# Round one of a two-branch attention kernel: the second tile's queries and chosen columns formed before the transposed queries, and three weight splits placed behind evacuations

## The reference

```python
xn = layernorm(x)
# branch 1: local attention, 16 query heads, 4 key heads, 32 wide
q, k, v = xn @ Wq.T + bq, xn @ Wk.T + bk, xn @ Wv.T + bv
q, k = rope(rmsnorm(q) * qn_w), rope(rmsnorm(k) * kn_w)
a = softmax(where(key > query or query - key > 64, -10000, q @ k.T * scale)) @ v
out1 = a @ Wo.T + bo
# branch 2: one shared key and value per token, chosen by a gate among 16 heads
gate = softmax(xn @ W_gate.T); idx = argmax(gate)
fq, fk, fv = split(xn @ W_qkv.T)
K, V = fk[head idx], fv[head idx] * max(gate)
out2 = softmax(causal(fq @ K.T / sqrt(32))) @ V      # 16 query heads
return x + out1 + out2
```

## Time and profile before

| what | value |
|---|---|
| runs (3) | 668.30, 668.74, 669.78 us; median 668.74 |
| profiled execution | 671.4 us, its span 669.5 us |
| PE busy | 637.4 us, 95% of the span |
| POOL, DVE, ACT busy | 66%, 68%, 54% |
| PE in its first 40th of the span (16.7 us) | 4 tenths busy |
| PE's granted clock, whole span | 0.993 |

### The profile page before, as it was taken

One profiled execution on the slowest core, in us unless ns is written; L12 is line 12 of the kernel. 1 busy time (PEld: TensorE's weight loads), 2 busy tenths in 40 slices (PEclk: granted clock), 3 DMA queues, 4 the chain that ended last, 5 costly groups with the idle time before them and its releaser, 6 DMA issues.

```text
span 669.5 us, 19210 instructions
## 1 busy us (share of the span) xinstructions
PE 637.4 (95%) x7432; PEld 509.8 (76%) x7432; DVE 455.8 (68%) x1184; ACT 361.7 (54%) x906; POOL 442.4 (66%) x384
## 2 busy tenths in 40 slices
PE   4699999999999999999999899999999999999997
PEld 3587788887888888888778677777777777777675
DVE  3966457657665675656664388887878787878454
ACT  5357355625544445535257455656565565656684
POOL 3876856368654749382895467776878687868730
PEclk9999999999999999999999899999999999999999
DMA  9524222241223133212216631503214131302011
GB/s 315 197 60 112 60 77 79 76 122 41 78 70 91 50 94 104 78 39 75 64 33 166 163 96 58 137 26 93 71 51 113 51 111 36 104 29 89 4 34 33
DMA packets 64939, 56.59 MB, mean 85 GB/s; under 512 B 6480, under 2 KB 48848, under 8 KB 64848
## 3 DMA queue, kind: packets, MB, share of 16 engines
q1 hardware_dynamic: 62704, 54.45, 27.9%
q10 hardware_dynamic: 2144, 0.93, 0.5%
HBM read 37.20 MB, written 17.89 MB: 82 GB/s over the span
## 4 chain that ended last, share of the span: by engine, by line
PE 88%; DVE 5%; ACT 2%; DMA 2%; issue 2%; SPq 0%; ACTq 0%; DVEq 0%
PE gemm L946 20%; PE s_ps L1055 12%; PE od_ps L1104 11%; PE st_ps L1088 10%; PE gemm L1032 7%; PE gemm L942 6%; PE od_ps L1118 5%; PE win L1006 4%; PE win L991 3%; PE s_ps L1127 2%; PE av L1018 2%; DMA raw<-w_tok 2%; PE av L1045 1%; PE tp L957 1%; PE tp L913 1%
## 5 line engine op out<-in xcount | busy, mean ns | idle before, releaser
L946 PE MATMUL gemm<-w_tok,xt 128*128 128x512 f32 (+1 forms) x768 | 184.0, 380 | 5.4 <-DVE g_exp L1188 2.2
L946 PEld LDWEIGHTS gemm<-w_tok,xt 128*128 128x128 f32 x768 | 129.6, 191 | 28.5 <-DVE g_exp L1188 2.7
L1055 PE MATMUL s_ps<-k_stack,w_tok 96*128 96x512 f32 (+2 forms) x336 | 100.0, 381 | 0.3 <-DVE x_res L1286 0.3
L1088 PE MATMUL st_ps<-w_tok,k_stack 98*128 98x512 f32 x288 | 98.9, 413 | 0.2 <-ACT p_loc L1545 0.2
L1545 ACT ACTIVATE p_loc<-st_ps 128x512 f32<-128x512 f32 x144 | 77.6, 599 | 35.9 <-PE st_ps L1088 34.7
L1321 DVE TENSOR_REDUCE picked_fk<-s_ps 128x1 f32<-128x512 f32 x112 | 72.3, 684 | 9.0 <-PE s_ps L1055 8.9
L1497 ACT ACTIVATE p_loc<-win,l_max 128x96 f32<-128x96 f32 x256 | 60.9, 390 | 31.1 <-DVE l_max L1260 31.1
L1055 PEld LDWEIGHTS s_ps<-k_stack,w_tok 96*128 96x128 f32 x336 | 54.9, 188 | 24.6 <-issue 8.8
L1642 POOL TENSOR_TENSOR rope_b<-qkv,sin_t 128x128 f32<-128x128 f32 (+1 forms) x32 | 27.5, 880 | 65.5 <-DVE qkv L1238 65.5
L1666 POOL TENSOR_TENSOR p_loc<-p_loc,l_rec 128x1536 f32<-128x1536 f32 x16 | 44.1, 2758 | 36.4 <-DVE l_rec L1272 36.4
L1324 DVE CUSTOM_DVE_ANT_0 s_ps<-s_ps,x_ln,picked_fk 128x128 f32<-128x128 f32 (+3 forms) x112 | 56.8, 555 | 9.7 <-PE s_ps L1055 9.7
(11 more groups left out here) (172 smaller groups left out, 1295.4 us busy)
## 6 DMA issues: line engine op xcount, KB each, us to landing
w_tok<-q_parts SPq DMA_DIRECT2D x72, 128.0 KB, 2.6
q_parts<-qt SPq DMA_DIRECT2D x120, 64.0 KB
x_ln<-x SPq DMA_DIRECT2D x8, 512.0 KB, 4.6
x_res<-x SPq DMA_DIRECT2D x16, 256.0 KB, 2.8
partial<-x_res SPq DMA_DIRECT2D x16, 256.0 KB, 2.3
w_tok<-partial SPq DMA_DIRECT2D x8, 512.0 KB, 5.2
raw<-w_tok SPq DMA_DIRECT2D x3, 1024.0 KB, 12.5
v_win<-v_rows SPq DMA_DIRECT2D x64, 48.0 KB, 2.2
```

Source lines behind the costliest of these rows:

```text
L946: i = e.matmul(g[:, 0:cols], xs[l][:, k, a * P:(a + 1) * P], w_tok_p[r][:, k, c0:c0 + cols], start=first, stop=last)
L1055: e.matmul(s_ps[bank][:, 0:cols], q_op[b][0:HALVES, i, h, :], k_stack[0:HALVES, b * S + c0:b * S + c0 + cols], start=True, stop=True).then ...
L1088: e.matmul(st_ps[k % ST_BANKS][:, :, :], k_stack[0:HALVES + 2, b * S + j * P:b * S + (j + 1) * P], q_op[b][0:HALVES + 2, i, :, :], start=T ...
```

## The change

Three edits. Round 0 has an order of its own: the units `q` 1, `fk` 1 and `fv` 1 come ahead of all four `qt`. The residuals of three pieces are put behind an evacuation on DVE: that of `fk` behind `kv_biased` of tile 0, that of `fv` behind `q_biased` of tile 0, that of `qt` behind `q_biased` of tile 1. And ACT's constants are issued in another order: the small activation with its table load comes right behind the identity's DMA; then rank and the bias of keys and values, rope table, norm weights, scale, and last the bias of the queries, for which `q_biased` of tile 0 now waits, while `kv_biased` waits for rank and its own part only.

```diff
-FIRST_UNITS = UNITS
+LO_BEHIND = {"fk": ("kvg", 0), "fv": ("q", 0), "qt": ("q", 1)}
+
+FIRST_UNITS = [("kvg", 0), ("q", 0), ("fk", 0), ("kvg", 1), ("fv", 0), ("q", 1), ("fk", 1), ("fv", 1), ("qt", 0), ("qt", 1),
+               ("qt", 2), ("qt", 3)]
...
+    late_lo = {}
...
                 do("w_hi", n)
-                do("w_lo", n)
+                if PIECES[n] in LO_BEHIND:
+                    late_lo[(0, *LO_BEHIND[PIECES[n]])] = n
+                else:
+                    do("w_lo", n)
             piece_ready[n] = p.busy(p.now, ("A", 1.9), ("V", 2.3)) + HOP
...
         do("kv_biased", n, a)
+        if (n, kind, a) in late_lo:
+            do("w_lo", late_lo.pop((n, kind, a)))
...
         do("q_biased", n, a)
+        if (n, kind, a) in late_lo:
+            do("w_lo", late_lo.pop((n, kind, a)))
...
                 if n == 0:
-                    lane.wait_ge(*M["bias_in"].of("all"))
+                    lane.wait_ge(*M["bias_in"].of("keys"))
...
                 g = gemm[plan.turn["bank", ("gemm", n, "q", a)]]
+                if (n, a) == (0, 0):
+                    lane.wait_ge(*M["bias_q_in"].of("all"))
...
         e.dma_start(idt[:, :], ident).then_inc(*M["ident_in"].did("all", inc=16))
+        lane.wait_ge(*M["filled"].of("half"))
+        e.activation(warm[:, :], minus_half[:, :], ACT.Exp).then_inc(*M["warmed"].did())
+        for dst, src in ((rank_t[:, :], rank), (bias[:, HD:N_QKV], b_qkv[:, HD:N_QKV])):
+            e.dma_start(dst, src.to_broadcast(dst.shape)).then_inc(*M["bias_in"].did("keys", inc=16))
         e.dma_start(rope_t[:, :, :, :], rope.rearrange("(t p) a d -> p t a d", p=P)).then_inc(
             *M["rope_in"].did(inc=16))
-        for dst, src in ((rank_t, rank), (bias, b_qkv)):
-            e.dma_start(dst[:, :], src.to_broadcast(dst.shape)).then_inc(*M["bias_in"].did("all", inc=16))
         for dst, src in ((norm_w[:, :, :, :].rearrange("p a b d -> p (a b d)"), w_norm), (scale_t[:, :], scale)):
             e.dma_start(dst, src.to_broadcast(dst.shape)).then_inc(*M["rope_in"].did("all", inc=16))
-
-        lane.wait_ge(*M["filled"].of("half"))
-        e.activation(warm[:, :], minus_half[:, :], ACT.Exp).then_inc(*M["warmed"].did())
+        e.dma_start(bias[:, 0:HD], b_qkv[:, 0:HD].to_broadcast([P, HD])).then_inc(*M["bias_q_in"].did("all", inc=16))
```

More of the change, by code:

```diff
@@ L708 @@
     "r_in0 r_in1 rs_mm rs_max r_hi r_lo r_mm r_t r_row r_row_lo rst_mm rp_exp rp_diag rp_pair rp_pair_v rpv rsum ro_r ro_mm ro_rec "
-    " ro_norm ro_out ro_out_v stored0 stored1 masked first_in first_mm first_max raw_used raw_in0 raw_in1 raw_in2 raw_in3 w_hi ident_in bias_in rope_in mask_in bias_o_in filled tables warmed"
+    " ro_norm ro_out ro_out_v stored0 stored1 masked first_in first_mm first_max raw_used raw_in0 raw_in1 raw_in2 raw_in3 w_hi ident_in bias_in bias_q_in rope_in mask_in bias_o_in filled tables warmed"
 ).split()
```

## The result

The changed kernel is **slower**: 676.94 us (676.47 to 677.45, 4 runs) against 668.52 (668.29 to 669.78, 4 runs), a ratio of 1.0106 with an interval of 1.0075 to 1.0136 (the quotient of the two medians is 1.0126). By the medians that is 8.4 us more, where 3.3 less were forecast. Before's four executions came out short: in the rounds of the experiments 105 executions of it range from 667.67 to 673.34 us with a median of 669.6, and against that the loss is 7.3 us; the ratio makes it 7.1. The profiled execution of after took 676.71 us with a span of 675.5; the one of before has a span of 669.5.

The account below looks back on a forecast made before the run. PE, busy 637.4 of 669.5 us, was taken as the bound, with only idle time and clock to win. Round one's loss of 7.43 us becomes 1.7 + 1.3 + 0.9 + 0.2 = 4.1, a gain of 3.3: 668.74 becomes 665.4, range 663.2 to 669.5.

Parts of the forecast that it names:

- replanned later rounds that eat the gain: Rounds after the first: their newly planned order takes back the gain, so the time stays the same; chance 0.10.
- Ahead of fv 0: PE in round one: 1.7 us of idle remain, from 23.0 to 24.7, until the pick of fk 0.
- Third idle time and its slow clock: PE ahead of qt 0 in the kernel before: 2.81 us of idle and 1.57 of slow clock go.
- Tile 0's products: POOL's two products for tile 0's queries: start near 23.7, held by the fv split, and take 3.67 us.
- q_t 0: PE at tile 0's transposed queries: waits 1.3 us for POOL's scaling, bounds 0 and 2.8, start near 34.7.
- Constants: ACT's DMA issues at the start: new order costs nothing; keys' bias bounded at 0 and 0.5 us.
- the clock falls anyway: Rival: idle times of 1.7, 1.3 and 0.9 us within 18 us slow PE's clock; price 1.57 us, 667.0; chance 0.15.
- Masks and scores: PE ahead of the scores, behind the wo split, layer norm and masks: 0.9 us of idle, bounds 0 and 2.
- Four qt in a row: Round one's four qt units, which need ACT while weights block it: 0.2 us added, bounds 0 and 2.3.
- slower rival: ACT becomes the wait of the four qt, twice 2.3 us plus the clock: 6.0 us against the gain, 671.4; chance 0.13.
- port rival: POOL's power excludes the qt split for its whole 3.54 us; PE waits 2.8 us at q_t 0: 668.4; chance 0.12.
- 7.43 us of idle time and slow clock: PE's loss in round one of the kernel before: 5.86 us idle ahead of fk 0, kvg 1, qt 0, plus 1.57 slow clock.

Follow-up runs that it names:

- E1: Changed kernel's round one, with the order of the kernel before from round two on: 671.47 us, 1.0031.
- E7: Changed kernel with the split of wo moved behind the pick of fk 1: 675.84 us, 1.0093.
- E8: E7's round one, with the later order of the kernel before: 670.55 us, 1.0006.
- E12: E10's round one with its own plan, so the changed kernel's later order: 676.91 us, 1.0108.
- E10: E9 with the split of fv moved from behind q_biased 0 to behind the pick of fk 0: 672.11 us, 1.0029.
- E4: Kernel before with only the planner's SLACK at 0.8 in place of 0.6, so another written order: 672.31 us, 1.0042.
- E5: Kernel before with only the constants' new order, units and splits as before: 671.02 us, 1.0019.
- E9: E8 with norm weights, scale and rope table issued ahead of rank and the keys' bias: 671.56 us, 1.0017.
- E13: Kernel before's order of units, the change's constants; splits behind: fk kv_biased 0, fv pick of fk 0, qt kv_biased 1; wo in its old place: 671.50 us, 1.0015.
- E6: E5 plus the splits of fk and fv moved behind the evacuations, the qt split in its old place: 669.31 us, 1.0000.
- E11: Kernel before's order of units everywhere, with all splits moved (wo late) and the tables' constants first: 670.41 us, 1.0010.
- E14: Changed kernel's order of units and constants, with all splits in their old places: 677.82 us, 1.0116.
- E3: Changed kernel with the planner's SLACK at 0.8 in place of 0.6, later rounds planned otherwise: 669.99 us, 1.0012.
- E15: E7 with the planner's SLACK at 0.8, so another later order: 668.16 us, 0.9972.
- E2: Kernel before's round one, with the changed kernel's order for later rounds and its constants: 681.66 us, 1.0187.

## Why the prediction was wrong

**The step that failed** is the last sentence of the sum: "The rest of the first stage is planned anew from other clock values; PE's idle time there has nothing that this change aims at, and I give it 1 us either way." That term measured +5.0 to +5.5 us (after against E1), +5.3 (E7 against E8) and +4.8 (E12 against E10). The list of rivals did hold "replanned later rounds that eat the gain", at 0.10, but bounded by the gain; with the size as measured it is a rival of the other side, slower, and the range's high end of 669.5 couldn't hold it. The mechanism: the order of rounds two to eight follows from the planner's clock at the end of round one, and the last round's attention falls differently into the last units. In the list of after the transposed queries of the last tile have 4 steps `gemm` behind them, in that of before 12. In the trace the projections end 5.5 us earlier than in E1 (367.6 against 373.1) and the last round's exponentials start 4.5 us later (357.29 against 352.75), so attention is left over with nothing beside it. In after, PE has 1.24 and 1.09 us of idle time at 376 to 380 us, with no unit left to fill them, and the clock falls behind them. A warning could have been read ahead without a chip: the planner's end of both kernels is there to be printed, 394.97 and 404.06. It overstates (E4: +9.4 for +2.8 us), but a change of 9 in it is not "1 us either way".

**The second error, about 5.4 us:** the other terms added up to a gain of 3.3 us, and round one came out as a loss. E1, with the old order behind it, is at 1.0031, 2.1 us *slower* than before. Either error alone puts the time beyond the range. By the terms:

- *Ahead of fk 0*: forecast none, measured none. fk 0 follows q 0 at once (36 matmuls in a row from 14.89). Right.
- *Ahead of fv 0*: forecast 1.7 us ended by the pick, measured 0.98 ended by the pick. The mechanism was right, and the size 0.7 too high: the split of fk began at 16.11 instead of 16.81, and everything behind it was earlier.
- *Third idle time and its slow clock*: gone from that place, as forecast. But a clock of 0.50 stands at 36 to 38 us, which the prediction had named as a sign of error.
- *Tile 0's products*: forecast to start near 23.7, held by the split of fv; measured 23.65. That is luck: the split ended at 22.22, and what ended last was POOL's own sine table (20.02 to 23.49), late because the scale was first used at 17.31 and the split had held the table.
- *q_t 0*: forecast 1.3 us of wait and a start of 34.7; measured 3.94 and 35.76. Two parts. PE came at 31.8 rather than 33.4, since it had lost less on the way; that alone only turns a gain into a wait. And POOL ended 1 us later than forecast, for another cause: the split of *wo*, not that of qt, stood in the scaling's way. The text had wo's split "at 35.0 to 37.2 behind the factors"; it began at 32.30. E7 removes that and gets 1.47 us of wait back.
- *Constants*: forecast none. Their order alone measured 1.0019 (E5), with an interval that just includes no change.
- *The clock*: the prediction had its first rival, "the clock falls anyway", on the sum of three short idle times. It fell, but behind one long idle time. The forecast price was 1.57 us; the rows of after give 1.6 (1.11 against 0.60 for the four transposes, 2.70 against 1.63 for six matmuls).
- *Masks and scores*: forecast 0.9 us of wait, and none stands ahead of the scores of tile 0 (42.15). Instead 0.58, 0.69 and 0.81 us stand at q_t, k_t and the scores of tile 1.
- *Four qt in a row*: forecast 0.2 us. Here a resource was left out. ACT's exponentials and a copy behind them hold the third qt's copy until 52.3, but then it waits for the store of the qt two before, and the fourth waits for such a store alone. Those stores are four DMA issues each on SP's queue, and the first began only at 48.12, though its qt was copied at 45.23: DVE's residual of it (47.63) stood behind the maxima of tile 0 (45.97, 1.75 us). SP of after:

```profile
48.12 4.71 SPq L1757 DMA_DIRECT2D q_parts<-qt  x8
52.87 2.76 SPq L1799 DMA_DIRECT2D v_win<-v_rows  x4
55.67 0.43 SPq L1768 DMA_DIRECT2D x_res<-x  x1
56.20 2.19 SPq L1757 DMA_DIRECT2D q_parts<-qt  x4
```

and ACT, whose third and fourth copies wait 0.87 and 2.71 us for it:

```profile
53.21 0.38 ACT L1478 ACTIVATE qt<-gemm 128x256 fp32r<-128x256 f32 x1 [0.87 <-DMA q_parts<-qt]
56.31 0.38 ACT L1478 ACTIVATE qt<-gemm 128x256 fp32r<-128x256 f32 x1 [2.71 <-DMA q_parts<-qt]
```

Four qt in a row put eight issues of 4.71 us together. A unit's matmuls then wait for the bank (57.20, 1.31 us), and once more at 61.58 (1.34), where DVE's evacuation is late. Before had waits of 0.26 and 1.28 us around its last two qt, so the place costs some 1.3 us more rather than 0.2. The slower rival had this place and only one of its two causes; no run isolates its share.

Together, PE's idle times behind 20 us and the slow clock come to 11.4 us in after up to 70 us (0.98, 3.94, 0.58, 0.69, 0.81, 0.15, 1.31, 1.34 and 1.6) and to 9.0 in before (5.86, 0.26, 1.28 and 1.57): 2.4 us more, near the 2.1 of E1.

*The port rival* (0.12 in the forecast): the trace of after decides it. The split of qt (29.67 to 31.95) ran 2.28 us inside the power's 3.54, neither longer, so a power that already runs doesn't exclude it. The Trainium skill ("SBUF — State Buffer", Who interferes with whom) has a DVE instruction with two inputs in SBUF contend with a GpSimd instruction that reads SBUF, and gives the shared pair of ports to whoever issues first "for the whole instruction". For a power that came first this trace disagrees, by 2.28 us of overlap. For a power that came second it agrees: `ln_y` of E7 took 2.75 us in place of 0.70 behind the split of wo. For the scaling it agrees too: 2.73 us in after, 1.26 in E7 where the split stands behind it.

**Why no repair of round one gained.** The prediction took the 7.43 us of idle time and slow clock as winnable at PE. But q_t 0 and q_t 1 each wait for a chain on POOL: two products, addition, power (3.54 us) and scaling per tile. In after its first tile runs from 23.65 to 35.70, 12 us, with the second right behind; without the split of wo in it (E7) it takes 10.6. What PE gained ahead of it came back as waits at q_t: 3.94 (E1), 2.44 + 2.47 (E8), 1.32 + 4.24 (E9), 3.42 (E13). In the kernel before the scaling ended at 36.91 and PE came at 37.66: PE was late enough by 0.75 us not to wait. That distance, and what POOL's own start moved, was there to be won, not 7.43. PE was the busiest engine on the page; in this one stage POOL stood right behind it.

That the chain's end is what bounds E8, E9 and E13 is read from their waits; a kernel with a shorter chain on POOL wasn't run. Nor are these repairs a clean test of it, for in each of them a split of DVE holds POOL by 1.4 to 2.1 us: ln_y ahead of tile 1's chain (E8), tile 1's products (E9), the scaling (E13). A place for wo's split in which it meets none of these, inside tile 1's power for one, was not tried, and it stays open what round one could gain with it.

**What stays open.** Which single due time makes this later order 5 us longer wasn't isolated. The traces show that it is lost between the exponentials of the last tile but two (334.40 against 336.65 in E1, still ahead) and those of the next tile (357.29 against 352.75), and then in the waits and the clock behind them, not which step set it up. And the last residual is a row of one execution each, while executions of one kernel differ by up to 5 us: in E6, E8 and E11, with before's later order, it comes 1.0 to 2.4 us earlier than in before's profile, yet the ratios are 1.0000, 1.0006 and 1.0010, all within the noise. 1.5 us of that is the slow clock of before's profiled execution.

## What to carry to other kernels

Where a program writes the instruction order, an edit at the start is two edits: print the order's own end for both versions, and measure the edit with the later order frozen, before its local gain is believed or dismissed. Before counting an engine's idle time as winnable, work out when the next engine's chain would be ready if the wait were gone: that distance, not the idle time, is the gain. And follow a step that is moved, with its stores and splits, to the queue that issues them and to the engine that they exclude: here the split of wo found something of POOL's to hold in most of the places that it was given.

## What the runs showed of the hardware that was not expected

- **A split begun while POOL's power runs isn't held; in the other meetings listed here the later one waits.** The power (128x20, 3.54 us) ran beside the whole split of qt (2.28 us) in after. The scaling (128x640, 1.26 alone) took 2.73, 3.03 and 2.71 behind the start of the split of wo in after, E5 and E13. A small power (128x2, 0.70 alone) took 2.75 behind the start of that split in E7. And where the scaling began first, by 0.05 us in E14, it took 1.27 and the split 3.37.
- **A small DMA's issue on ACT's queue isn't constant.** The scale's issue took 0.50 us in before (from 3.88) and 1.88 us in after (from 5.09). From the start of the issue it landed 12.4 and 12.1 us later, and was first used at 16.40 and 17.31.
- **The clock at the end of the first stage goes mostly with the order of work, but not only.** From 360 to 400 us it is 0.88 to 0.95 in all four profiles with the new later order behind its own round one, where PE had idled 1.24 and 1.09 to 1.94 us. It is 1.00 in those of E1, E5, E6, E8 to E11 and E13, with the old later order, but 0.91 from 360 to 380 in before's, which has the same order and the same wait of 1.53 us there. E3 and E15 share a later order too, and have 1.00 and 0.91 there.
- **The same wait at the same place isn't always followed by the slow clock.** E2 and E5 have the same round one. Ahead of qt 0 PE idled 1.91 us in E2, and its clock was at 0.50 from 31 us on (24 matmuls in 4.46 us); in E5 it idled 1.89, and the clock stayed at 1.00 (the same 24 in 3.01).
